# Three float32 products of a transformer kernel rewritten as float32r products of two-part operands, with new static orders

## The reference

```
x += xattn0(LN(x), ctx)   # cross attention, output norm; self attention (16 heads of 16), output norm;
                          # gelu(h @ fi_w + fi_b) @ fo_w, output norm
x += experts(LN(x))       # 8 experts of width 256, two picked per token by a sigmoid router, relu squared
x += xattn1(LN(x), ctx)   # cross attention with 10 prefix keys and a mask
x += ffn(LN(x))           # h = x @ (tern(w_fc) * scale).T + gate * (x @ v.T @ fast_b.T @ u.T)
                          # y = relu(h)^2 @ (tern(w_proj) * scale).T
```

## Time and profile before

| | |
|---|---|
| Times of three runs | 1098.97, 1097.04, 1104.51 us |
| Span of the profiled execution | 1094.8 us (the profile gives no other time of that execution) |
| PE busy | 1019.2 us, 93%, 7648 products or transposes |
| DVE busy | 782.0 us, 71% |
| ACT busy | 607.7 us, 56% |
| POOL busy | 331.8 us, 30% |
| Mean granted TensorE clock | 0.975 of full speed |

### The profile page before, as it was taken

The page is one execution under the profiler, slowest core; times in us unless marked ns, Lnnn a source line. Parts: engine busy times, 40 slices in busy tenths (PEclk is TensorE's granted clock), DMA queues, the critical chain, the costliest instruction groups (busy, mean ns, idle before and its releaser), DMA issues.

```text
span 1094.8 us, 20748 instructions
## 1 busy us (share of the span) xinstructions
PE 1019.2 (93%) x7648; PEld 601.0 (55%) x7648; DVE 782.0 (71%) x1337; ACT 607.7 (56%) x1191; POOL 331.8 (30%) x724
## 2 busy tenths in 40 slices
PE   5999989999999999999988898989898999999998
PEld 3675666433333333333344665648677676576865
DVE  4786577689999999999723747546536756887565
ACT  2665554478888888888853123131222456556543
POOL 3422111001010343344103334373366433530000
PEclk9999999889999999999998997999999999999999
DMA  7302221451221212212125100021344301100000
GB/s 213 70 16 88 87 68 66 144 188 44 75 71 48 70 49 69 79 45 70 47 67 191 34 15 10 20 77 44 101 155 132 100 31 49 44 25 1 16 18 26
DMA packets 97578, 75.67 MB, mean 69 GB/s; under 512 B 49806, under 2 KB 87483, under 8 KB 97223
## 3 DMA queue, kind: packets, MB, share of 16 engines
q1 hardware_dynamic: 94407, 65.95, 20.0%
q0 software_dynamic: 3072, 8.39, 2.4%
HBM read 42.94 MB, written 30.93 MB: 67 GB/s over the span
## 4 chain that ended last, share of the span: by engine, by line
PE 65%; DVE 10%; DMA 8%; issue 5%; POOL 4%; ACT 4%; SPq 3%; POOLq 0%; DVEq 0%; ACTq 0%
PE OUT L855 15%; PE TR L855 14%; PE OUT L1090 9%; PE TR L861 8%; PE TR L1079 7%; DMA head_q<-MT 7%; PE OUT L1079 3%; PE TR L931 3%; PE SCR L915 2%; POOL dispatched L2038 2%; SPq L697 2%; ACT PTS L1298 2%; PE SCR L908 2%; DVE small L1486 1%; PE OUT L861 1%
## 5 line engine op out<-in xcount | busy, mean ns | idle before, releaser
L1555 DVE TENSOR_REDUCE small<-SCR 128x1 f32<-128x1024 f32 x256 | 308.5, 1223 | 26.2 <-PE SCR L962 20.3
L1396 ACT ACTIVATE shared<-TR 128x512 f32<-128x512 f32 x352 | 200.1, 597 | 38.8 <-PE TR L1079 30.7
L962 PE MATMUL SCR<-head_k,head_q 48*128 48x512 f32 x512 | 193.9, 456 | 2.7 <-DVE P L1531 2.7
L1090 PE MATMUL OUT<-shared,HM 128*32 128x256 f32 x2048 | 165.3, 394 | 1.2 <-ACT shared L1396 0.4
L1079 PE MATMUL TR<-head_q,head_k 51*128 51x512 f32 x352 | 149.7, 463 | 0.9 <-issue 0.6
L1919 POOL TENSOR_SCALAR small<-small 128x1 f32<-128x1 f32 x112 | 27.7, 247 | 346.7 <-DVE small L1487 344.5
L855 PE MATMUL TR<-xT,fifo 128*128 128x512 f32 x224 | 105.8, 629 | 1.1 <-ACT xT L1276 1.0
L1396 ACT ACTIVATE shared<-OUT 128x512 f32<-128x512 f32 x160 | 95.8, 599 | 19.3 <-PE OUT L1079 17.6
L1079 PEld LDWEIGHTS TR<-head_q,head_k 51*128 51x128 f32 x352 | 60.6, 186 | 76.4 <-ACT shared L1396 56.5
L1276 ACT ACTIVATE xT<-TR 128x256 f32<-128x256 f32 x96 | 35.4, 381 | 111.5 <-PE TR L861 108.6
L1090 PEld LDWEIGHTS OUT<-shared,HM 128*32 128x32 f32 x2048 | 41.4, 108 | 93.1 <-ACT shared L1396 57.6
(11 more groups left out here) (241 smaller groups left out, 1860.3 us busy)
## 6 DMA issues: line engine op xcount, KB each, us to landing
pieces<-pieces SPq DMA_DIRECT2D x16, 512.0 KB, 2.7
HM<-dispatched SPq DMA_DIRECT2D x46, 128.0 KB
expert_out<-HM SPq DMA_DIRECT2D x46, 128.0 KB
dispatched<-HB SPq DMA_DIRECT2D x6, 768.0 KB, 4.0
head_q<-pieces SPq DMA_DIRECT2D x32, 128.0 KB
head_k<-pieces SPq DMA_DIRECT2D x32, 128.0 KB
shared<-in_L_ffn_w SPq DMA_DIRECT2D x4, 1024.0 KB, 12.0
x<-TOK SPq DMA_DIRECT2D x16, 128.0 KB, 1.7
```

What stands on the lines that cost most here:

```text
L962: ins = nc.tensor.matmul(SQ[kt % 2][:, hf, :], QX[n % 2][rows, kt * 128:(kt + 1) * 128], KX[n % 2][rows, hf * 512:(hf + 1) * 512], start=T ...
L1090: ins = nc.tensor.matmul(PV[32 * g:32 * g + 32, 0:256], VH[:, n % 2, kt, :], PTB[:, kt % 2, g * 256:(g + 1) * 256], start=(kt == 0), stop= ...
L1396: nc.scalar.activation(PTB[:, kt % 2, hf * 512:(hf + 1) * 512], ring_bank("t_scores", n, kt, hf), ACT.Exp, scale=DH ** -0.5).then_inc(st_d ...
L1555: nc.vector.tensor_reduce(nm[:, n % 2, kt:kt + 1], SQ[kt % 2].rearrange("p h n -> p (h n)"), AX, ALU.max, negate=True).then_inc(sq_done.se ...
```

## The change

Self QKV, GELU up and ternary up become sums of float32r products of operands in two parts: `hi` is the value rounded to float32r, `lo` the rest.

- QK, SV: three products for each half of the features (hi x hi, hi x lo, lo x hi). POOL splits the three weights in a new step WS. LT of part A becomes LA: PE transposes into an OUT bank, ACT copies it rounded (XAH), DVE subtracts that from the bank (XAL).
- FI: the same with LX (XGH, XGL); POOL splits the GELU weights during heads 1 to 8.
- FC: the ternary weights stay unscaled, so they are exact in float32r, and relu takes the scale (`scale=wscale`). Two products for each half (weights x hi, weights x lo) and one for the low-rank term over all 128 rows: `fcL` holds the parts of u times gate over scale, `YS` the parts of the 16 middle values for the block, made by a new step YP from `GX` (fast_b.T @ v in parts). LT of part C becomes LW (XWH, XWL). UT moves to part C and transposes the split u weights; GG and FL go.
- T, QK, FI and FC become steps of one bank each (`T.3.2`, `QK.0.1`), so the lists can place other steps between them. PZ clears the pad columns of P, whose space the GELU parts use before.
- Both orders are rewritten as a whole; the rules of the schedules are fitted. Three places of the new lists stand in the diff: the end of ORDER_A, the first ternary blocks and the end of ORDER_C.

```diff
 ORDER_A = """
...
+SV.13 MX.1.1 MX.1.2 MT
+QK.3.0 QK.3.1 MX.1.3 QK.3.2 MX.1.4 QK.3.3 MX.1.5 MX.1.6 MX.1.7 SV.14 SV.12 SV.15
...
 ORDER_C = """
...
+L3.8 T.7.1 CB.10 T.7.2 FC.0.1 YS.41 FC.0.2 DM.10 YS.43 YS.42 T.7.3 FC.0.3 CG.12 FC.0.4 PV.7 FC.0.5 VW.1 L3.10 RX.10
+CB.12 L3.11 FC.0.6 FC.0.7 PJ.5 YS.44 CG.14 YS.45 QP.2 S.8 E.8 DM.12 RX.12 CG.13 FP.0 FP.1 CT.6 S.9 CB.13 RX.11 PN.5
...
+CT.15 PN.13 FP.8 PJ.15 PN.14 LW.13 PN.15 FP.10 LW.14 LW.15 FP.9 YP.3 FP.11 FC.3.0 FC.3.1 FC.3.2 FC.3.3 FC.3.4 FC.3.5
+FC.3.6 FC.3.7 FP.12 FP.13 FP.14 FP.15
...
 @block.tensor
-            def self_qk(k):
-                at.block_copied("LT", k)
-                for w in (sq, sk):
-                    for m in range(KD):
-                        at.feature_major(w, xTb, m)
+            def self_input(t):
+                pe.wait_ge(tok_ready.sem, tl.after(tok_ready, "PN", t))
+                bank = out_bank(tl)
+                transposes(bank, [TOK[:, t % 2, k * 128:(k + 1) * 128] for k in range(KD)]).then_inc(out_full.sem, 1)
+
+            def self_qk(k, e):
+                pe.wait_ge(out_done.sem, tl.after_block(out_done, "LA", k))
+                pe.wait_ge(ws_ready, 1)
+                j, c = e // KD, slice(e % KD * 128, e % KD * 128 + 128)
+                bank = tr_bank(tl)
+                product(bank, [(w[:, j, f, c], x[:, f, :]) for f in range(KD)
+                               for w, x in ((WH, XAH), (WH, XAL), (WL, XAH))]).then_inc(tr_full.sem, 1)
...
-                at.token_major(xTb, sv, t, range(KD))
+                product(bank[:, 0:D], [(x[:, f, c], w[:, 2, f, :]) for f in range(KD)
+                                       for x, w in ((XAH, WH), (XAH, WL), (XAL, WH))]).then_inc(out_full.sem, 1)
...
-                        at.feature_major(fi, xTb, m)
+                    product(bank, [(w[:, f, c], x[:, f, :]) for f in range(KD)
+                                   for w, x in ((FIH, XGH), (FIH, XGL), (FIL, XGH))]).then_inc(tr_full.sem, 1)
...
+                def low_rank_middle(k):
+                    pe.wait_ge(out_done.sem, tl.after_block(out_done, "LW", k))
+                    pe.wait_ge(g_ready, 1)
+                    bank = tr_bank(tl)
+                    product(bank, [(GX[:, f, :, :].rearrange("p c r -> p (c r)"), x[:, f, :])
+                                   for f in range(KD) for x in (XWH, XWL)]).then_inc(tr_full.sem, 1)
+
+                def ternary_up(k, m):
+                    at.copied("UT")
+                    pe.wait_ge(y_ready.sem, tl.after(y_ready, "YP", k))
+                    ms_ = slice(m * 128, (m + 1) * 128)
+                    bank = tr_bank(tl)
+                    product(bank, [(fcT[:, f, ms_], x[:, f, :]) for f in range(KD) for x in (XWH, XWL)]
+                            + [(fcL[:, ms_], YS[:, :])]).then_inc(tr_full.sem, 1)
...
 @block.scalar
+            def self_input(t):
+                bank = OUT[:, tl.slot(out_full, 2), :]
+                act.wait_ge(out_full.sem, tl.next(out_full))
+                c = t % BT * 128
+                nc.scalar.activation(XAH[:, :, c:c + 128], bank[:, 0:256].rearrange("p (k n) -> p k n", k=KD), ACT.Copy)\
+                    .then_inc(xa_ready.sem, 1)
...
+                def low_rank_weights():
+                    for hf in range(2):
+                        bank = emptied(tl)
+                        nc.scalar.activation(fcL[0:4 * R, hf * 512:(hf + 1) * 512], bank[0:4 * R, :], ACT.Copy)
+                        nc.scalar.activation(fcL[4 * R:128, hf * 512:(hf + 1) * 512].rearrange("p (a n) -> p a n", a=4),
+                                             identf[4 * R:128, :].unsqueeze(1).to_broadcast([128 - 4 * R, 4, 128]),
+                                             ACT.Copy, scale=0.0).then_inc(tr_done.sem, 1)
...
+                def low_rank_middle(k):
+                    bank = emptied(tl)
+                    nc.scalar.activation(YF, bank[2 * R:3 * R, :], ACT.Copy)
+                    nc.scalar.activation(YS[:, :], bank, ACT.Copy).then_inc(tr_done.sem, 1)
...
 @block.vector
+            def self_input(t):
+
+                bank = filled(tl)
+                dve.wait_ge(xa_ready.sem, tl.next(xa_ready))
+                c = t % BT * 128
+                signal_out(tl, nc.vector.tensor_tensor(
+                    XAL[:, :, c:c + 128], bank[:, 0:256].rearrange("p (k n) -> p k n", k=KD),
+                    XAH[:, :, c:c + 128].bitcast(F32), ALU.subtract))
...
+                def low_rank_middle(k):
+                    dve.wait_ge(tr_done.sem, tl.next(tr_done))
+                    low = YS[2 * R:3 * R, :]
+                    nc.vector.tensor_tensor(low, YF, low.bitcast(F32), ALU.subtract).then_inc(y_ready.sem, 1)
...
 @block.gpsimd
+            def self_weights():
+
+                pool.wait_ge(d_aw, 16 * 4)
+                for j, w in enumerate((sq, sk, sv)):
+                    chain(nc.gpsimd.tensor_copy(WH[:, j, :, :], w))
+                    ins = nc.gpsimd.tensor_tensor(WL[:, j, :, :], w, WH[:, j, :, :].bitcast(F32), ALU.subtract)
+                ins.then_inc(ws_ready, 1)
...
             for n in range(NH):
+                if n == 1:
+                    pool.wait_ge(d_fifo, 16 * 2)
+                if 1 <= n < 1 + 4 * KD:
+                    k, c = divmod(n - 1, 4)
+                    part = (slice(None), k, slice(c * 256, (c + 1) * 256))
+                    chain(nc.gpsimd.tensor_copy(FIH[part], fi[part]))
+                    ins = nc.gpsimd.tensor_tensor(FIL[part], fi[part], FIH[part].bitcast(F32), ALU.subtract)
+                    if n == 4 * KD:
+                        ins.then_inc(fi_ready, 1)
```

More of the change, by code:

```diff
@@ L85 @@
     "E": dict(exp=1),
-    "T": dict(tr=4),
+    "T": dict(tr=1),
     "PV": dict(tr=1),
@@ L123 @@
     "RX": dict(res=1),
-    "FC": dict(tr=MF, low=MF, top=MF),
+    "LW": dict(out=1, hi=1),
+    "YP": dict(tr=1, low_rank=1),
+    "FC": dict(tr=1, low=1, top=1),
     "FP": dict(out=1),
@@ L186, in attention_order @@
             before((a, t), (b, t + 1))
         if t + 2 in tiles:
-            before(("T", t), ("S", t + 2))
-            before(("LT", t), ("PN", t + 2))
+            before(("T", t, 3), ("S", t + 2))
+            before((last, t), ("PN", t + 2))
     for t in tiles:
+        for g in range(3):
+            before(("T", t, g), ("T", t, g + 1))
         if t // BT * BT > tiles[0]:
@@ L210, in schedule_a @@
     order, before = parsed(ORDER_A)
-    attention_order(before, range(T))
+    attention_order(before, range(T), "LA")
+    before(("WS",), ("LA", 0))
     for t in range(T):
@@ L232, in schedule_a @@
     for k in range(BLOCKS):
-        before(("QK", k), ("LH", 0))
+        before(("QK", k, 2 * KD - 1), ("LH", 0))
+    for k in range(T // BT):
+        for e in range(2 * KD):
+            if (k, e) > (0, 0):
+                before(("QK", k, e - 1) if e else ("QK", k - 1, 2 * KD - 1), ("QK", k, e))
     before(("LH", 0), ("LH", 1))
@@ L245, in schedule_c @@
     order, before = parsed(ORDER_C)
-    attention_order(before, range(T))
+    attention_order(before, range(T), "LW")
     for t in range(T):
@@ L264, in schedule_c @@
         before(("FN", t), ("CB", t))
[L265 to L269 removed]
+        before(("FO", t), ("FC", 0, 0))
+        before(("SO", t), ("LW", 0))
+        before(("FO", t), ("LW", 0))
+        before(("LW", t), ("YP", t // BT))
+        before(("L2", t), ("UT",))
+        before(("RT", t), ("FC", 0, 0))
+        before(("DS", t), ("FC", 0, 0))
+        before(("ST", t), ("T", 0, 0))
+    for i in range(B * NS):
+        first = i - i % NS % 4
+        if i > first:
+            before(("XT", first), ("XT", i))
+        if first % NS:
+            before(("XT", first - 4), ("XT", first))
     for i in range(2, B * NS):
@@ L1145, in _ @@
                         .then_inc(tr_full.sem, 1)
+            pe.wait_ge(d_low, 16 * 4)
+            bank = tr_bank(tl)
+            for k in range(KD):
+                ins = nc.tensor.matmul(bank[:, k * R:(k + 1) * R], v_sb[:, k * 128:(k + 1) * 128], fbT, start=True, stop=True)
+            ins.then_inc(tr_full.sem, 1)
             pe.wait_ge(diag_ready, 1)
@@ new lines, in self_qk @@
+            def self_qk(k, e):
+                if e == 0:
+                    if k == 0:
+                        act.wait_ge(d_const, 16 * 6)
+                    act.wait_ge(d_pieces, k * 4 * 16 + DC)
+                bank = emptied(tl)
+                bias = cols["sq_b" if e < KD else "sk_b"][:, e % KD:e % KD + 1]
+                act.wait_ge(pc_ready.sem, tl.back(pc_ready, 1))
+                tl.next(pc_ready)
+                nc.scalar.activation(PC[e][:, 0, :], bank, ACT.Identity, bias=bias)
+                nc.scalar.activation(RR[:, e % 2, :], bank, ACT.Identity, bias=bias).then_inc(tr_done.sem, 1)
@@ new lines, in ternary_up @@
+                def ternary_up(k, m):
+                    bank = emptied(tl)
+                    act.wait_ge(l_ready.sem, tl.back(l_ready, 1))
+                    r = RR[:, tl.slot(l_ready, 2), :]
```

(4 more changed lines are left out.)

432 lines of the change are left out of this document (237 added, 195 removed).

## The result

The changed kernel takes **1128.3 us** (median of 4 runs, 1126.6 to 1134.7) against 1099.6 us: ratio 1.0274, 95% interval 1.0234 to 1.0315. The profiled execution took 1126.62 us with a span of 1124.6. The forecast of 1076 and its range miss it, and so does the sign.

The account below looks back on a forecast made before the run. PE was taken to set the time nearly everywhere. First stage -8, GELU -7.7, experts and heads 0, last attention -6.3, end -0.7: -22.7 us, span 1094.8 to 1072.1, plus 4.2 gives 1076 us; range 1058 to 1091.

Parts of the forecast that it names:

- PE's terms: Changes in PE's own work over all stages, with float32r steps at 0.235 us: 29.8 us less.
- that rival: Weights in the open: 560 float32r products each pay 0.10 us for their weight load, adding 56 us: 1132 us; chance 0.02.
- They delay what stands behind a block's last tile: The 48 added DVE subtractions, 0.417 us each, 20 us in all, over three stages with 57 to 80 us idle DVE.
- 4 x 0.42 for GELU: Four added subtractions ahead of the GELU blocks, 1.7 us lost in a stage forecast at -7.7 us.
- 1.5 us for the last attention: New waits there as DVE nears PE's load: 1.5 us added (ends 0 and 8), stage -6.3 us.
- 4 us in the first stage: At the stage's end PE, with about 22 us of work, waits 4 us for DVE's 26 (ends 0 and 7).
- Steps per tile are the same: Experts, heads and weights would take the same time: 0 us (ends -4 and +4).
- YP at 3.8 us on PE in all, and at 1.3 to 1.7 us at the end: YP: 0.94 us of PE work in each of four blocks; in the last, another 0.4 to 0.8 us uncovered.
- 3 us back at the heads' start: With FL gone, half of some 6 us lost to the low clock there would return (ends 0 and 6).
- DVE waits in line behind ACT: Rival: each LA, LX, LW holds DVE's queue about 0.9 us for PE and ACT, 43 us in all: 1119 us; chance 0.06.
- The new orders idle more: Rival: the rewritten orders add a fifth, 14 us, to PE's 75.6 us of waits: 1090 us; chance 0.17.

Follow-up runs that it names:

- e6: Kernel before, its orders and products unchanged, with only the 48 input steps put in, through an OUT bank: 1142.3 us, ratio 1.0417.
- e5_tr_ring_old: Changed arithmetic in the order of before, with the 48 input transposes in a TR bank that ACT frees: 1111.2 us, ratio 1.0128.
- e8: e5_tr_ring_old with the 48 subtractions on GpSimd instead of VectorE: 1123.1 us, ratio 1.0213.
- e1: Changed kernel's arithmetic in the order of before: 1138.2 us, ratio 1.0357.
- e9: Kernel before, its orders and products unchanged, with the 48 input steps put in through a TR bank: 1123.7 us, ratio 1.0202.
- e12: e11 with YP's work left out too: 1101.0 us, ratio 1.0019.
- e11: e5_tr_ring_old with ternary up's third product reading another tile, so that no step waits for YP: 1108.7 us, ratio 1.0098.
- e7: e5_tr_ring_old with each YP some steps ahead of its FC block in the C order: 1115.5 us, ratio 1.0144.
- e10: e8 and e7 together: 1126.4 us, ratio 1.0234.

## Why the prediction was wrong

*PE's terms: right.* 30 us were forecast and 30 measured; 0.235 us a step was taken, 0.23 measured. Three GELU blocks, each begun at half clock before and after, fell from 15.7 to 16.0 us to 12.9 to 13.4; the fourth, with 6 us at half clock and a wait inside, stayed at 15.5. The last ternary block, forecast at 11.5, ran in 9.9. By the Trainium skill's rule (TensorE: Matmul & The Clock Gate, Back-to-back issue gap) a step would be 0.216; the trace stays with the longer one. The weights are not in the open either, so that rival is out, and it is luck that its 1132 us come nearest to the measured time.

*"They delay what stands behind a block's last tile", costed at 4 x 0.42 for GELU, 1.5 us for the last attention, 4 us in the first stage: the step that failed.* The prediction priced the 48 subtractions as DVE work, 0.42 us each, with idle DVE to hide them. It never asked which PSUM ring they write to. The diff said it: "LX": dict(tr=1) became dict(out=1, xhi=1). A TR bank is free when ACT has copied; the OUT bank is free when DVE has got round to the subtraction, and every other OUT step of PE queues behind that. The 48 steps by themselves cost 46 us in the order of before (e6), more than all that the products save. The bank is 24 of them. The later start of the products that need the low part, and ACT's and DVE's added work, are the other 22. In the new orders the steps were not taken out by themselves, so this split is shown for the order of before alone. The prediction also had PE idle for long in GELU's stretch only (23 us); the earlier trace rows has 21.4 us in the first stage too, where it counted on DVE's free time.

*"Steps per tile are the same", for experts and heads.* The heads bear it out (-1.4 us). In the experts a further 5 us came with the new order, beyond the bound of 4.

*YP at 3.8 us on PE in all, and at 1.3 to 1.7 us at the end.* Its chain through ACT and DVE was counted once, at the kernel's end. In e5_tr_ring_old it is waited for in the open four times, and it is worth some 12 us.

*The clock.* The prediction gave 3 us back at the heads' start. It was not got: the granted clock is 0.55 from 227 to 237 us, without any FL, behind 2.9 us of idle time from 218 on. In the whole span the work loses 13 us more to the clock than before. That more waits precede the work is the likely reason, but the clock was not tested alone, and it follows the idle time only roughly: e8's clock is 0.943 with 117.8 us idle, the changed kernel's 0.956 with 122.0.

*The rival nearest to what happened* is "DVE waits in line behind ACT", 1119 us. It has the right steps and the wrong engine. DVE's waits behind ACT in LA, LX and LW sum to 14 us in the changed kernel (2.2, 3.6 and 8.4), not 43. It is PE that waits, for the bank and for the block. "The new orders idle more" expected added idle time, 14 us where 46 came; with these steps the orders reduce it (128.6 us idle in e1, 122.0 in the changed kernel), though they add waits of their own at the start and in the experts.

*What stays open.* From e9 to e12 PE's work falls by the products' saving, some 38 us, and the time by 20 us only. Where it goes can be read stage by stage from e9, e5_tr_ring_old and e11. GELU's stretch gets all of it: 180.1 us in e9, 166.7 in e5_tr_ring_old, its blocks 3 us shorter each. The stretches between the blocks stay (30.3, 37.4 and 29.1 us in e9, 30.3, 36.7 and 29.1 in e5_tr_ring_old, against 24.9, 35.9 and 25.9 before); the changed products are not in them, the input steps are. In the first stage PE is busy for 10.5 us less in e5_tr_ring_old than in e9, and idle for 6.3 us more, so 4.2 us arrive. In the last part, without the wait for YP, 6.3 us arrive (241.5 us in e9, 235.2 in e11). What binds in these two was not found, nor how much of it is the clock. The first stage also varies from one execution to another: it took 218.7 and 227.9 us in two kernels that are alike there (e5_tr_ring_old, e7), 218.5 and 222.3 in two others (e8, e10). So the 11.3 us of the changed kernel's first stage are uncertain by most of their size.

## What to carry to other kernels

When a step is given another bank ring, price the time for which the bank is held, up to the last reader's place in its in-order queue, and not the reader's own duration. In the order of before, 48 subtractions of 0.42 us on an engine that is idle for 29% of the span cost 46 us here, 24 of them because two banks were shared with all other steps of the tile. In the longest waits for a low part most of the time was other tiles' steps ahead in the list, not the subtraction itself. And a product that gets cheaper pays only where its inputs are early: put the added input step alone into the old kernel first, since that one run, 46 us against a forecast saving of 30 on PE, would have told the sign.

## What the runs showed of the hardware

In one stretch of GELU the granted clock fell during waits and stayed low into the work behind them. It was 1.00 from 580 to 588 us of the changed kernel; PE then waited 2.40 us for a norm, and from 590 to 600 us (PE busy for 5.98 of 10 us) the clock was 0.50. The float32r steps of the block that starts at 596.46 are 0.43 us apart until 600.03, 0.23 from then on:

```profile
590.00:600.00 10.00, 5.98 (x16) 4.11 (x17) 5.22 (x14) 3.40 (x6) 2.89 (x5) 0.50 0.79 264
600.00:610.00 10.00, 9.48 (x41) 7.40 (x39) 0.00 (x0) 4.72 (x8) 3.77 (x6) 1.00 0.00 0
```

So a late block pays twice, once for the wait and once for its first products at half speed (3.6 us here, 3 to 6 in the four blocks). The second payment is not new: the four blocks of the kernel before took 15.4 to 16.0 us where 32 records at full clock take 13.90.
